# Head sums per token tile, squares of x from row-major x, and an early load of the second batch's rows

## The chip, the cores and the metric

One core of a Trainium2 chip runs the kernel; the other cores have nothing to do with it. The metric is the time of one execution on the device in microseconds (us), as the median of several. Lower is better. The engines are called PE (TensorE), DVE (VectorE), ACT (ScalarE), POOL (GpSimd) and SP (SyncE, which issues most of the DMAs).

## What is computed

Two cross-attention layers over 16 batches of 512 tokens with 256 features. The first layer is the one that the change touches:

```python
def _L0_xattn_ref(x_tokens, ctx, ctx_index_per_token, gamma_q, gamma_kv, Wq, Wk, Wv, Wo):
    # B=16, T=512, K=64, D=256, H=16 heads of hd=16
    q = split(rmsnorm(x_tokens, gamma_q) @ Wq.T)
    kn = rmsnorm(ctx, gamma_kv)
    k = split(kn @ Wk.T)
    v = split(kn @ Wv.T)
    ctx_pos = jnp.arange(K)[None, None, :]
    mask = (jnp.abs(ctx_pos - ctx_index_per_token[:, :, None]) <= 1)[:, None]
    scores = jnp.einsum('bhqd,bhkd->bhqk', q, k) / math.sqrt(hd)
    w = jnp.square(jax.nn.relu(scores))
    w = jnp.where(mask, w, 0.0)
    denom = jnp.maximum(w.sum(-1, keepdims=True), EPS_DEN)
    out = jnp.einsum('bhqk,bhkd->bhqd', w / denom, v)
    return x_tokens + out.reshape(B, T, D) @ Wo.T
```

The second layer takes that result as its queries: it projects, applies gelu, scores it against the 64 context rows of its batch, takes a softmax, adds the result to its input and applies a layer norm.

## The kernel before, in words

Because of the mask a token looks at three context rows only: that of its own index (CENTRE), the next (UP) and the one before (DOWN). The kernel picks these rows by matmuls with a one-hot matrix. The queries of layer 0 are not normalised: w stays unscaled, and the floor under the denominator is scaled instead, by the sum of squares of each token's x. So for each token and head three products are needed (query times picked key, summed over the 16 features of the head), and for each token the sum of x squared.

**Head sums.** The products lie in the tile `qk`, features over partitions (two groups g of 128) and 512 tokens along the free axis, one slice of 1024 elements per shift. `head_sums` (L571 to L579) sums over the features of a head with a selection matrix of 32 columns. The PE array is used in four groups of 32 columns: three of them take one shift each, the fourth takes the squares of x (`xsq`), and each streams 512 tokens. The result fills bank 0 of the PSUM: quarter s of the partitions holds shift s, the last quarter the floor. ACT moves it to `s_sb` with a Relu and adds a small bias in the floor's row (L1049), PE turns it by four transposes of 128x128 (L640) so that tokens lie on partitions, ACT squares the three shifts in place (L1061), and DVE sums them to `den`, takes the maximum with the floor in PSUM (`dcl`, L1327), the reciprocal (L1329) and the weights `wn` (L1331). `xsq` is made by ACT in `square_x` (L1004 to L1007): one Square over the whole 128x1024 slice of `x_ring`, where x lies features over partitions.

**The pipeline.** `steps` (L216) runs 16 steps. In a step five batches are under way: e is loaded, a gets its queries and picked keys, f its weights and picked values, b is projected to the second layer's queries and scored, n gets its softmax, layer norm and output. The order on each engine is written out by hand, in a function `step` per engine. What matters here is one round of PE and DVE. At the end of a PE step stand `head_sums(a)` and then, as the first thing of the next step, the eight transposes of the attended values (L635), which wait for DVE's sum of the three shifts (L1305, semaphore `sum_ready`). Behind them come the transposes of `s_sb` (L640), two transposes of the softmax (L648), half of the queries (L498 to L500), the output matmuls (L670), picked values UP (L549) and the projection of b (L498 to L500 on `o_hi`, `o_lo`). DVE waits for the projection in the second of its two residual additions (L1347, semaphore `xp_mm`). After that DVE makes `xp_lo` (L1350), the attended values (L1270, L1356), the products of the next batch (L1259), CENTRE values (L1270), the maxima of the scores (L1376) and again the sum L1305.

**The start.** PE computes keys and values for all 16 batches, two per tile t (0 to 7). ACT rounds them (L991, `round_keys_values`), DVE computes the remainder (L1221), and SP moves half of each tile across partitions (`cross`, L262 to L267, "the crossing"). ACT's list there is fixed: four sums of squares of the context rows (L963), `square_x(0)`, tiles 4 and 5, x of batch 1, tiles 6 and 7. After tile 7, DVE splits the weights of the second layer's values (`v_lo`, L1298), for which PE waits. SP issues the loads of x (`load`, L257 to L260), the crossings, and four shifted copies of the keys and values per batch (`shifted`, L269 to L279).

## Time and profile before

| | |
|---|---|
| median of 3 runs | 348.92 us (348.28 to 348.96) |
| the profiled execution, whole | 349.19 us |
| its span, first to last instruction | 347.4 us |
| PE busy in the span | 332.7 us, 96% |
| DVE busy | 307.8 us, 89% |
| ACT busy | 242.2 us, 70% |
| POOL busy | 169.7 us, 49% |
| mean granted clock of PE | 0.988 |
| DMA | 37.96 MB, mean 109 GB/s |

The span has three parts: the start to about 53 us, thirteen steps that repeat nearly alike, one every 18.2 us, and the end from about 307 us. Busy shares are averages over all three. A matmul's end is modelled in the profile, and matmuls overlap, so PE counts as busy up to the modelled end even where its next instruction waits. PEld is PE's loading of stationary operands, which can run ahead of the matmuls. Instructions that only wait or issue a DMA are not busy time. Times in the rows are microseconds from the start of the span.

### The profile page before, as it was taken

To read this page: it belongs to the slowest core of one execution; us is meant where nothing else is said; L and a number is where in the kernel's file an instruction comes from. 1 tells how busy PE (TensorE), PEld (TensorE's weight loads), DVE (VectorE), ACT (ScalarE), POOL (GpSimd) and SP (SyncE) were. 2 spreads that over 40 slices of the span, in tenths; PEclk is the share of its full clock that TensorE was granted. 3 is DMA by queue.
4 is the path that set the end of the run, shared out by engine and by line. 5 is a ranking of instruction groups with operands and counts; after the bars stand their busy time and mean duration, and the time that the engine had idled before them with its cause. 6 is when DMAs were issued, how large, how long until landed. Compare 5 with 4: busy or idle time off the path is not lost.

```text
span 347.4 us, 5599 instructions
## 1 busy us (share of the span) xinstructions
PE 332.7 (96%) x1930; PEld 240.7 (69%) x1930; DVE 307.8 (89%) x486; ACT 242.2 (70%) x486; POOL 169.7 (49%) x203
## 2 busy tenths in 40 slices
PE   7999999999999999999999999999999999999980
PEld 3575778868686767676868677776767686857750
DVE  1689598999999999999999989999999999999766
ACT  4599433486868695959595959596877868685752
POOL 4315020025656473839283747474747566444424
PEclk9899999999999999999999999999999999999997
DMA  7975615903232222323141414141414132010103
GB/s 238 315 219 149 199 57 131 248 17 129 83 117 94 102 98 79 109 66 126 63 149 60 152 61 151 62 150 62 150 63 144 67 133 80 2 60 2 60 0 122
DMA packets 21819, 37.96 MB, mean 109 GB/s; under 512 B 2144, under 2 KB 8288, under 8 KB 21792
## 3 DMA queue, kind: packets, MB, share of 16 engines
q1 hardware_dynamic: 18816, 29.48, 27.2%
q0 software_dynamic: 2016, 7.34, 6.1%
q10 hardware_dynamic: 960, 0.79, 0.7%
q8 instruction: 15, 0.25, 0.3%
q14 instruction: 12, 0.10, 0.1%
HBM read 16.77 MB, written 8.39 MB: 72 GB/s over the span
## 4 chain that ended last, share of the span: by engine, by line
PE 79%; DVE 13%; ACT 3%; DMA 2%; issue 1%; ACTq 0%; DVEq 0%
PE ps L498 12%; PE ps L499 12%; PE ps L500 12%; PE ps L577 7%; PE ps L549 7%; PE ps L543 6%; PE ps L635 4%; PE ps L670 4%; PE ps L752 4%; PE ps L743 4%; DMA vfd<-wv0T 2%; PE ps L530 2%; PE ps L640 2%; DVE qkp L1259 2%; DVE kv L1221 2%
## 5 line engine op out<-in xcount | busy, mean ns | idle before, releaser
L1259 DVE TENSOR_TENSOR qkp<-ps,bufs 128x1024 f32<-128x1024 f32 x48 | 55.7, 1215 | 0.9 <-PE ps L543 0.8
L377 POOL TENSOR_TENSOR x_lo<-x_ring,x_hi 128x1024 fp32r<-128x1024 f32 x16 | 38.0, 2373 | 37.7 <-ACT x_hi L998 37.7
L418 POOL TENSOR_TENSOR bufs<-bufs,lng_twice 128x1024 f32<-128x1024 f32 x14 | 33.8, 2411 | 28.3 <-ACT bufs L1038 26.2
L1076 ACT ACTIVATE xp_hi<-bufs 128x512 fp32r<-128x512 f32 x28 | 17.7, 632 | 41.1 <-DVE bufs L1347 41.1
L391 POOL TENSOR_TENSOR mean_gap<-stats 128x4 f32<-128x4 f32 x14 | 2.8, 198 | 72.0 <-DVE stats L1336 65.2
L1270 DVE TENSOR_TENSOR ps<-ps,wn 128x1024 f32<-128x1024 f32 x31 | 37.9, 1224 | 0.0
L420 POOL TENSOR_TENSOR bufs<-bufs,lnb_row 128x1024 f32<-128x1024 f32 x14 | 33.3, 2378 | 1.1
L577 PE MATMUL ps<-qkp,cst 128*32 128x512 f32 x192 | 30.7, 598 | 0.0
L577 PE MATMUL ps<-bufs,cst 128*32 128x512 f32 x64 | 30.5, 598 | 0.0
L1002 ACT ACTIVATE bufs<-ps 128x512 f32<-128x512 f32 x32 | 19.2, 603 | 16.1 <-PE ps L500 16.0
L498 PE MATMUL ps<-x_hi,wh_q 128*128 128x512 f32 x64 | 26.6, 415 | 0.0
L1038 ACT ACTIVATE bufs<-ps,nbias,half_rstd 128x256 f32<-128x256 f32 x52 | 25.0, 562 | 0.2
L499 PE MATMUL ps<-x_hi,wl_q 128*128 128x512 f32 x64 | 25.1, 392 | 0.0
L500 PE MATMUL ps<-x_lo,wh_q 128*128 128x512 f32 x64 | 25.1, 392 | 0.0
L498 PE MATMUL ps<-xp_hi,wh_q 128*128 128x512 f32 x60 | 23.8, 396 | 0.1
L498 PE MATMUL ps<-o_hi,wh_o 128*128 128x512 f32 x60 | 23.5, 392 | 0.0
L499 PE MATMUL ps<-xp_hi,wl_q 128*128 128x512 f32 x60 | 23.5, 391 | 0.0
L499 PE MATMUL ps<-o_hi,wl_o 128*128 128x512 f32 x60 | 23.5, 391 | 0.0
L500 PE MATMUL ps<-xp_lo,wh_q 128*128 128x512 f32 x60 | 23.5, 391 | 0.0
L500 PE MATMUL ps<-o_lo,wh_o 128*128 128x512 f32 x60 | 23.4, 389 | 0.0
L1347 DVE TENSOR_TENSOR bufs<-ps,x_ring 128x512 f32<-128x512 f32 x28 | 19.2, 686 | 3.9 <-PE ps L500 3.9
L1270 DVE TENSOR_TENSOR qkp<-ps,wn 128x1024 f32<-128x1024 f32 x16 | 19.4, 1210 | 3.4 <-PE ps L549 3.3
(257 smaller groups left out, 933.3 us busy)
## 6 DMA issues: line engine op xcount, KB each, us to landing
x_ring<-xT SPq DMA_DIRECT2D x16, 512.0 KB, 3.5
out<-bufs POOLq DMA_DIRECT2D x14, 512.0 KB, 3.4
idx_ring<-idx SPq DMA_DIRECT2D x16, 256.0 KB, 3.9
wkv_lo<-kv SPq DMA_DIRECT2D x32, 126.0 KB
kvs<-kv SPq DMA_DIRECT2D x30, 126.0 KB
vfd<-bufs SPq DMA_DIRECT2D x8, 256.0 KB, 4.5
qkp<-ctxT SPq DMA_DIRECT2D x2, 512.0 KB, 6.8
kv<-kv_cross SPq DMA_DIRECT2D x8, 128.0 KB, 4.1
```

Of the source, the lines that this page charges most:

```text
L377: G.tensor_tensor(x_lo[:, :, :], x_ring[:, e % RING, :, :], f32_view(x_hi[:, :, :]), ALU.subtract).then_inc(xl_ready, 2)
L418: G.tensor_tensor(zo, zn, lng_twice[:, :].unsqueeze(1).broadcast_to([P, TT, D]), ALU.mult).then_inc(zg_ready, 1)
L420: G.tensor_tensor(zo, zo, lnb_row[:, :].unsqueeze(1).broadcast_to([P, TT, D]), ALU.add).then_inc(zo_ready, 1)
L498: mm(o, hi, m_hi, start=start, stop=False)
L499: mm(o, lo, m_hi, start=False, stop=False)
L500: last = mm(o, hi, m_lo, start=False, stop=stop)
L543: i = mm(ps[:, bank0 + g, :], shift_rows(a, s, 0)[:, g * P:(g + 1) * P], onehot[:, a % 2, :], start=True, stop=True)
L549: i = mm(ps[:, bank0 + j // 2, (j % 2) * D:(j % 2 + 1) * D], onehot[:, f % 2, j * P:(j + 1) * P], shift_rows(f, s, 1), start=True, stop=True)
L577: i = mm(ps[32 * s:32 * s + 32, 0, :], sum_sel[:, g if s < SHIFTS else 2, :], qk[:, s, g, :] if s < SHIFTS else xsq[:, g, :], start=(g == ...
L1038: i = A(zn[:, j, :], out_rows(j), ACT.Identity, bias=nbias[:, j:j + 1], scale=half_rstd[:, j:j + 1])
L1259: V.tensor_tensor(qk[:, s, :, :], ps[:, bank0:bank0 + 2, :], q0, ALU.mult).then_inc(qk_ready, 1)
L1270: V.tensor_tensor(dst.rearrange("p a (h d) -> p (a h) d", d=HD), picked(bank0).rearrange("p a (h d) -> p (a h) d", d=HD), wn[:, s, :, :].r ...
```

## The change

`head_sums` is cut along the tokens instead of along the shifts: the four column groups take the four tiles of 128 tokens, and each matmul streams the three shifts of its tile, 3 x 128 = 384 columns. The squares of x are no longer an operand of PE. In their place x is loaded a second time, in rows (tokens over partitions, new tensor `x`, new tile `x_rows`, 512 KB for each batch), and ACT squares it in four instructions of 128x256 with an accumulator output into `floor`. DVE then adds the small constant to `floor` and takes the maximum with `den` in one instruction. The Relu moves 384 columns instead of 512 and has no bias, there are three transposes instead of four (one per shift), and the weights lie in another order in PSUM.

`load_rows(i)` on SP waits until the squares of the batch before are done. `load_rows(0)` stands behind the context rows in the start, `load_rows(1)` between the third and the fourth crossing, and the others at the end of SP's step, behind the shifted copies. `square_x` waits for the rows and no longer for the head sums of the batch before.

```diff
-C_ID, C_SEL, C_POS, C_EPS, C_END = 0, 128, 224, 225, 226
+FLOOR_SCALE = (16.0 * EPS_DEN / D) ** 0.5
+C_ID, C_SEL, C_POS, C_END = 0, 128, 192, 193
...
-        xsq, q0, xpT, q1T = (bufs[:, n, :].rearrange("p (c t) -> p c t", c=DC) for n in (0, 3, 4, 5))
+        q0, xpT, q1T = (bufs[:, n, :].rearrange("p (c t) -> p c t", c=DC) for n in (3, 4, 5))
+        x_rows = bufs[:, 0, :].rearrange("p (j d) -> p j d", j=TT)
+        floor = sb("floor", [P, 2, TT])
...
-        by_token = ps[:, 0, :].rearrange("p (j r) -> p j r", j=TT)
-        w = by_token[:, :, 0:32 * SHIFTS].rearrange("p j (s h) -> p s j h", h=32)[:, :, :, 0:H]
-        den_floor = by_token[:, :, 96:97]
+        by_shift = ps[:, 0, 0:SHIFTS * P]
+        w = by_shift.rearrange("p (s j h) -> p s j h", s=SHIFTS, h=32)[:, :, :, 0:H]
...
+            def load_rows(i):
+                if i > 0:
+                    sp.wait_ge(floor_ready, TT * i)
+                sp.dma_start(x_rows, x[i].rearrange("(j p) d -> p j d", p=P)).then_inc(rows_in, 16)
...
             context_rows()
+            load_rows(0)
             weight(raw["v1"], wv1, wv1_in)
...
             cross(3)
+            load_rows(1)
             cross(4)
...
                     shifted(e)
+                if e is not None and e >= 2:
+                    load_rows(e)
...
             def head_sums(a):
                 pe.wait_ge(qk_ready, 3 * a + 3)
-                pe.wait_ge(xsq_ready, a + 1)
                 for g in range(DC):
-                    for s in range(SHIFTS + 1):
-                        i = mm(ps[32 * s:32 * s + 32, 0, :], sum_sel[:, g if s < SHIFTS else 2, :],
-                               qk[:, s, g, :] if s < SHIFTS else xsq[:, g, :], start=(g == 0), stop=(g == DC - 1))
+                    for j in range(TT):
+                        i = mm(ps[32 * j:32 * j + 32, 0, 0:SHIFTS * P].rearrange("p (s t) -> p s t", s=SHIFTS), sum_sel[:, g, :],
+                               qk[:, :, g, j * P:(j + 1) * P], start=(g == 0), stop=(g == DC - 1))
                 i.then_inc(s_mm, 1)
...
-                    for j in range(TT):
-                        i = nc.tensor.transpose(ps[:, 0, j * P:(j + 1) * P], s_sb[:, j * P:(j + 1) * P], ident)
+                    for s in range(SHIFTS):
+                        i = nc.tensor.transpose(ps[:, 0, s * P:(s + 1) * P], s_sb[:, s * P:(s + 1) * P], ident)
...
             def square_x(a):
-                if a > 0:
-                    act.wait_ge(s_mm, a)
-                A(xsq, x_ring[:, a % RING, :, :], ACT.Square).then_inc(xsq_ready, 1)
+                act.wait_ge(rows_in, 16 * a + 16)
+                if a > 1:
+                    act.wait_ge(dcl_ready, a - 1)
+                for j in range(TT):
+                    A(x_rows[:, j, :], x_rows[:, j, :], ACT.Square, scale=FLOOR_SCALE,
+                      accum_out=floor[:, a % 2, j:j + 1]).then_inc(floor_ready, 1)
...
-                    A(s_sb[:, :], ps[:, 0, :], ACT.Relu, bias=den_eps).then_inc(s_cp, 1)
+                    A(s_sb[:, 0:SHIFTS * P], by_shift, ACT.Relu).then_inc(s_cp, 1)
...
-                    V.tensor_tensor(dcl[:, :, :], den[:, :, :], den_floor.broadcast_to([P, TT, H]), ALU.max).then_inc(dcl_ready, 1)
+                    dve.wait_ge(floor_ready, TT * f + TT)
+                    V.scalar_tensor_tensor(dcl[:, :, :], floor[:, f % 2, :].unsqueeze(2).broadcast_to([P, TT, H]), 16.0 * EPS_DEN * EPS_RMS,
+                                           den[:, :, :], ALU.add, ALU.max).then_inc(dcl_ready, 1)
```

The same edits are made in the code for the last batch. How the instructions stand now is shown at three places. The first is PE at the end of a step: the last rows of the scores, the head sums (`32x512` is 32 output rows, 512 columns) and the first transposes of the next step. Before:

```order
L756 MATMUL ps<-cst,scT 128x128 [waits scT_cp]
L756 MATMUL ps<-cst,scT 128x128
L577 MATMUL ps<-qkp,cst 32x512 [waits xsq_ready,qk_ready]
L577 MATMUL ps<-qkp,cst 32x512 x2
L577 MATMUL ps<-bufs,cst 32x512
L577 MATMUL ps<-qkp,cst 32x512 x3
L577 MATMUL ps<-bufs,cst 32x512
L635 MATMUL ps<-cst,qkp 128x128 [waits sum_ready]
L635 MATMUL ps<-cst,qkp 128x128 x7
L640 MATMUL ps<-cst,s_sb 128x128 [waits s_cp]
```

The same place now, with the line numbers of the changed kernel:

```order
L766 MATMUL ps<-cst,scT 128x128 [waits scT_cp]
L766 MATMUL ps<-cst,scT 128x128
L587 MATMUL ps<-qkp,cst 32x384 [waits qk_ready]
L587 MATMUL ps<-qkp,cst 32x384 x7
L645 MATMUL ps<-cst,qkp 128x128 [waits sum_ready]
L645 MATMUL ps<-cst,qkp 128x128 x7
L650 MATMUL ps<-cst,s_sb 128x128 [waits s_cp]
L650 MATMUL ps<-cst,s_sb 128x128 x2
```

Still eight matmuls in four column groups, each of 384 columns now, and three transposes of `s_sb` in place of four; the wait of the turn for `sum_ready` stays where it was.

The second place is ACT in the start: the sums of squares of the context rows, the squares of x of batch 0, and the rounding of tile 4. Before:

```order
L963 ACTIVATE scT,cms<-bufs 128x256 [waits ctx_in]
L963 ACTIVATE scT,cms<-bufs 128x256 [waits cms_done] x3
L1007 ACTIVATE bufs<-x_ring 128x1024
L991 ACTIVATE kv<-ps,crs 64x512 [waits crs_done,kv_mm]
L991 ACTIVATE wh_q<-ps,crs 64x512
```

Now:

```order
L973 ACTIVATE scT,cms<-bufs 128x256 [waits ctx_in]
L973 ACTIVATE scT,cms<-bufs 128x256 [waits cms_done] x3
L1019 ACTIVATE bufs,floor<-bufs 128x256 [waits rows_in]
L1019 ACTIVATE bufs,floor<-bufs 128x256 x3
L1001 ACTIVATE kv<-ps,crs 64x512 [waits crs_done,kv_mm]
L1001 ACTIVATE wh_q<-ps,crs 64x512
```

One Square has become four with a wait for the loaded rows, ahead of the same rounding.

The third place is SP in a middle step, now: the load of x and of the indices, the four shifted copies, the rows.

```order
L261 DMA x_ring<-xT 128x2x512 [waits x_in,idx_in,onehot_ready,xp_ready]
L262 DMA idx_ring<-idx 128x512
L285 DMA wkv_lo<-kv 63x512 [waits kvs_in_1,vg_mm,kv_in_2,kvs_zero_1]
L286 DMA wkv_lo<-kv 63x512
L285 DMA wkv_lo<-kv 63x512
L286 DMA wkv_lo<-kv 63x512
L267 DMA bufs<-x 128x4x256 [waits floor_ready]
```

The last row is new; the six before it stand as they did.

## Rows read from the trace of the kernel before

**Rows 1.** The profile's page: the chain that ended last, by engine.
```profile
PE 79%; DVE 13%; ACT 3%; DMA 2%; issue 1%; ACTq 0%; DVEq 0%
```

**Rows 2.** One step by engine: stretch, length, busy time of each engine, clock, DMA.
```profile
core 0: us, PE busy (x) PEld busy (x) DVE busy (x) ACT busy (x) POOL busy (x), PEclk, DMA share, GB/s
...
144.04:162.27 18.23, 18.23 (x115) 13.27 (x118) 17.22 (x27) 13.84 (x29) 10.79 (x14) 1.00 0.31 101
```

**Rows 3.** Waits: engine, line, releaser: us in total, times, longest us.
```profile
PEld ps L635 <- DVE qkp L1305: 11.6, 13, 0.9
```

**Rows 4.** Timeline, DVE, one step: start, duration, line, operation, count, idle before.
```profile
144.63 1.21 DVE L1305 TENSOR_TENSOR qkp<-ps,qkp 128x1024 f32<-128x1024 f32 x1
...
148.81 0.22 DVE L1327 TENSOR_TENSOR dcl<-den,ps 128x64 f32<-128x64 f32 x1
...
153.56 0.69 DVE L1347 TENSOR_TENSOR bufs<-ps,x_ring 128x512 f32<-128x512 f32 x1 [0.26 <-PE ps L500]
154.16 1.48 DVE L1350 TENSOR_TENSOR xp_lo<-bufs,xp_hi 128x512 fp32r<-128x512 f32 x2
...
162.81 1.21 DVE L1305 TENSOR_TENSOR qkp<-ps,qkp 128x1024 f32<-128x1024 f32 x1
```

**Rows 5.** Timeline, PE, the same step.
```profile
144.85 0.60 PE L577 MATMUL ps<-qkp,cst 128*32 128x512 f32 x3
...
145.28 0.61 PE L577 MATMUL ps<-qkp,cst 128*32 128x512 f32 x3
...
145.90 1.09 PE L635 MATMUL ps<-cst,qkp 128*128 128x128 f32 x8
146.83 0.60 PE L640 MATMUL ps<-cst,s_sb 128*128 128x128 f32 x4
147.26 0.38 PE L648 MATMUL ps<-cst,enf 128*128 128x128 f32 x2
...
153.13 0.39 PE L500 MATMUL ps<-o_lo,wh_o 128*128 128x512 f32 x1
```

**Rows 6.** Timeline, PE, the step before the repeating ones: last head sums.
```profile
52.45 0.60 PE L577 MATMUL ps<-qkp,cst 128*32 128x512 f32 x3
```

**Rows 7.** Timeline, PEld, the same place: what is loaded behind the head sums.
```profile
52.99 1.59 PEld L530 LDWEIGHTS ps<-wf_raw,bufs 128*128 128x128 f32 x8 [0.84 <-issue]
```

**Rows 8.** Timeline, ACT, in the middle step.
```profile
149.56 1.05 ACT L1007 ACTIVATE bufs<-x_ring 128x1024 f32<-128x1024 f32 x1
153.33 0.63 ACT L1076 ACTIVATE xp_hi<-bufs 128x512 fp32r<-128x512 f32 x1 [2.72 <-DVE bufs L1347]
```

**Rows 9.** Timeline, ACT, in the start.
```profile
23.35 0.42 ACT L963 ACTIVATE scT<-bufs 128x256 f32<-128x256 f32 x1
...
23.89 0.42 ACT L963 ACTIVATE scT<-bufs 128x256 f32<-128x256 f32 x1
...
24.31 1.04 ACT L1007 ACTIVATE bufs<-x_ring 128x1024 f32<-128x1024 f32 x1
25.87 0.69 ACT L991 ACTIVATE kv<-ps,crs 64x512 fp32r<-64x512 f32 x1 [0.52 <-POOL crs L373]
```

**Rows 10.** The chain that ended last, in order of time, in the start.
```profile
35.34 0.70 DVE v_lo L1298
...
36.08 0.50 PE ps L498
```

**Rows 11.** DMA in the start, stretches as in rows 2.
```profile
14.00:16.00 2.00, 2.00 (x6) 1.04 (x5) 1.85 (x3) 0.92 (x3) 0.97 (x1) 0.83 1.08 342
16.00:18.00 2.00, 2.00 (x11) 1.62 (x10) 1.97 (x6) 1.95 (x3) 0.00 (x0) 1.00 0.41 106
```

**Rows 12.** Timeline, POOL, around the same middle step.
```profile
135.97 0.20 POOL L407 TENSOR_TENSOR nbias<-nmean,half_rstd 128x4 f32<-128x4 f32 x1
...
143.46 2.38 POOL L377 TENSOR_TENSOR x_lo<-x_ring,x_hi 128x1024 fp32r<-128x1024 f32 x1
...
154.16 0.74 POOL L407 TENSOR_TENSOR nbias<-nmean,half_rstd 128x4 f32<-128x4 f32 x1
```

More of the change, by code:

```diff
@@ L43, in xattn_pair @@
         ident = cst[:, C_ID:C_ID + P]
-        sum_sel = cst[:, C_SEL:C_SEL + 96].rearrange("p (g c) -> p g c", g=3)
+        sum_sel = cst[:, C_SEL:C_SEL + 64].rearrange("p (g c) -> p g c", g=DC)
         pos = cst[:, C_POS:C_POS + 1]
-        den_eps = cst[:, C_EPS:C_EPS + 1]
         vec = sb("vec", [P, 5, DC])
@@ L134, in xattn_pair @@
             "vec_in", "cst_in", "wk1_in", "wkv_in", "wq0_in", "wv1_in", "wf1_in", "w1_in", "ln_in", "x_in", "idx_in"))
+        rows_in = sem("rows_in")
         ctxT_in = [sem("ctxT_in0"), sem("ctxT_in1")]
@@ L145, in xattn_pair @@
         kv_first = sem("kv_first")
-        onehot_ready, xsq_ready, xh_ready, xl_ready = map(sem, ("onehot_ready", "xsq_ready", "xh_ready", "xl_ready"))
+        onehot_ready, floor_ready, xh_ready, xl_ready = map(sem, ("onehot_ready", "floor_ready", "xh_ready", "xl_ready"))
         q0_mm, q0_cp, kg_mm, qk_ready, s_mm, s_cp, sT_mm, w_ready = map(sem, (
@@ L773, in last_weights @@
                 pe.wait_ge(s_cp, LAST + 1)
-                for j in range(TT):
-                    i = nc.tensor.transpose(ps[:, 0, j * P:(j + 1) * P], s_sb[:, j * P:(j + 1) * P], ident)
+                for s in range(SHIFTS):
+                    i = nc.tensor.transpose(ps[:, 0, s * P:(s + 1) * P], s_sb[:, s * P:(s + 1) * P], ident)
                 i.then_inc(sT_mm, 1)
@@ L1059, in step @@
                     act.wait_ge(sT_mm, f + 1)
-                    by_row = w.rearrange("p s j h -> p j s h")
+                    by_row = w.rearrange("p s j h -> p (s j) h")
                     A(by_row, by_row, ACT.Square).then_inc(w_ready, 1)
@@ L1113, in last_sums @@
                 act.wait_ge(s_mm, LAST + 1)
-                A(s_sb[:, :], ps[:, 0, :], ACT.Relu, bias=den_eps).then_inc(s_cp, 1)
+                A(s_sb[:, 0:SHIFTS * P], by_shift, ACT.Relu).then_inc(s_cp, 1)
             def last_squares():
                 act.wait_ge(sT_mm, LAST + 1)
-                by_row = w.rearrange("p s j h -> p j s h")
+                by_row = w.rearrange("p s j h -> p (s j) h")
                 A(by_row, by_row, ACT.Square).then_inc(w_ready, 1)
@@ L1399, in last_weights @@
                 dve.wait_ge(den_ready, LAST + 1)
-                V.tensor_tensor(dcl[:, :, :], den[:, :, :], den_floor.broadcast_to([P, TT, H]), ALU.max).then_inc(dcl_ready, 1)
+                dve.wait_ge(floor_ready, TT * LAST + TT)
+                V.scalar_tensor_tensor(dcl[:, :, :], floor[:, LAST % 2, :].unsqueeze(2).broadcast_to([P, TT, H]), 16.0 * EPS_DEN * EPS_RMS,
+                                       den[:, :, :], ALU.add, ALU.max).then_inc(dcl_ready, 1)
                 dve.wait_ge(dcl_ready, LAST + 1)
@@ L1601 @@
     arrays = {
-        "xT": a["x"].transpose(0, 2, 1), "ctx": ctx, "ctxT": ctx.T, "idx": a["itok_BxS_0_255"],
+        "xT": a["x"].transpose(0, 2, 1), "x": a["x"], "ctx": ctx, "ctxT": ctx.T, "idx": a["itok_BxS_0_255"],
         "vectors": np.stack([a[n].reshape(DC, P).T for n in ("L0_xattn_gamma_q", "L0_xattn_gamma_kv", "L1_xattn_bq",
```

4 lines of the change are left out of this document (1 added, 3 removed).

## The prediction

> **What bounds the kernel now.** I read four views, from coarse to fine: the page, the waits, the stretches, and the timelines of one step. The page's chain gives PE 79% of the span [rows 1], and in a middle step PE counts as busy for all 18.23 us of its stretch, against 17.22 us of DVE [rows 2]. Read alone, this says that every microsecond taken from PE is a microsecond won. The waits say otherwise at one place: in 13 of the steps the loading of weights for the turn of the attended values (L635), right behind the head sums, ends a wait for DVE's sum L1305 [rows 3]. The timelines show how tight this is. The sum runs from 144.63 for 1.21 us, so it ends at 145.84, and L635 starts at 145.90, 0.06 us later [rows 4, 5].
>
> Was PE ready then anyway? The last group of four head sums starts at 145.28 [rows 5]. One step earlier in the program the same head sums are followed by work that waits for nobody: there the last group starts at 52.45 and the next weights are loaded at 52.99, 0.54 us later [rows 6, 7]. So PE was ready for L635 at 145.28 + 0.54 = 145.82, and DVE let it go at 145.90. The two engines meet here almost to the instant, and DVE is the later one.
>
> From there I follow the loop that sets the period. PE works from L635 (145.90) to the end of the projection's last matmul, 153.13 + 0.39 = 153.52: 7.62 us. DVE, which had stood idle for 0.26 us, starts its second residual addition at 153.56 [rows 4, 5]. From there to the end of the next sum (162.81 + 1.21 = 164.02) DVE needs 10.46 us. With the two hand-overs of 0.04 and 0.06 us the round is 7.62 + 0.04 + 10.46 + 0.06 = 18.18 us, which is the distance of the sums, 162.81 - 144.63 [rows 4]. **The head sums are not in this loop.** They run while DVE does its 10.46 us. PE's other loop, in which they are, is as long only by coincidence.
>
> **The change part by part.**
>
> Head sums: the four column groups start together, and such groups of four follow each other at 145.28 - 144.85 = 0.43 us [rows 5]. With 384 columns for 512 I take three quarters, 0.32 us. Four groups per batch save 0.43 us. Bounds: 0 if a group's time does not follow the columns (its moving operand now is three runs of 128), 0.43 if it does; I take 0.43 since the columns are what it streams. In the 13 steps that wait at L635, PE now arrives 0.43 us earlier and waits that much longer: nothing won. In the step before them it counts, because no one waits for DVE there [rows 6, 7]: PE is on the path from 36.08 [rows 10] until the first of the residual additions that wait for it. So 0.43 us, once.
>
> Transposes of `s_sb`: four take 147.26 - 146.83 = 0.43 us [rows 5], one of them 0.11. They lie behind the wait, inside PE's 7.62 us, so the one that goes shortens the loop: 13 steps and the one before, 14 x 0.11 = 1.54 us. What would be late next there is DVE: it had 0.26 us idle before the second addition [rows 4], so it is ready when PE comes 0.11 earlier, even if nothing else moves. Two more of these transposes go off the path for nothing: batch 0's before 36.08, where PE waits for `v_lo` [rows 10], and the last batch's, where the chain has left PE for DVE and ACT.
>
> Relu over 384 columns, no bias: its result is wanted by the transposes L640 only, behind eight others. Shorter, never later: 0.
>
> `square_x`, middle steps: one Square of 1.05 us becomes four of 128x256 with an accumulator. Such instructions follow each other at 23.89 - 23.35 = 0.54 us where they wait for one another, and the last is followed by the next instruction after 24.31 - 23.89 = 0.42 us [rows 9]. So four take 1.7 to 2.2 us, 0.6 to 1.1 more. Behind them on ACT stands the rounding of the second layer's queries, `xp_hi`, before which ACT idles 2.72 us, waiting for DVE [rows 8]. That covers it. Were this cover gone, `xp_hi` would be late by the excess and `xp_lo` on DVE with it, inside the loop. 0.
>
> `square_x(0)`, start: the same 0.64 to 1.12 us stand ahead of the rounding of tile 4, and there ACT idled only 0.52 us, waiting for POOL [rows 9]. The rounding comes 0.12 to 0.60 us later, and DVE's remainders and `v_lo`, for which PE waits at 36.08 [rows 10], can be late by all of it or by nothing, as DVE still has the products of batch 0 to do. Bounds 0 and +0.60; I take +0.10, near the low end, since these four do not wait for one another and so go at 0.42.
>
> DMAs: `load_rows(0)` puts 512 KB into SP's queue ahead of four weights. The queue's engines are full until 16 us (342 GB/s in 14 to 16) and idle by more than half after that (106 GB/s in 16 to 18) [rows 11]; 512 KB at 342 GB/s are 1.5 us. The weights behind it land that much later; the first of them is wanted by the split that ends in `v_lo` at 35.34 [rows 10]. The first copies of keys and values are issued at that time too, and PE wants the shifted ones some microseconds later. Bounds 0 and +1.5; I take 0, since the queue drains before these copies are all issued. `load_rows(1)` waits for ACT's squares between two crossings, where SP waits for later tiles anyway; nothing is queued behind it that could have gone. In the middle steps the rows are the last DMA of SP's step, and ACT wants them a whole step later. 0.
>
> DVE: `dcl` (0.22 us at 148.81 [rows 4]) becomes one instruction with two operations and reads the floor from SBUF. Its wait is for squares a step old. Between it and the loop's hand-over lies the 0.26 us of idle time, so up to that it costs nothing in the steps, and once, at the end, whatever it is longer. The sums over shifts now stride 128 words in place of 32. Bounds 0 and +0.3 in all; I take 0.
>
> One rule speaks against this edit. At 154.16 DVE runs `xp_lo`, with both inputs in SBUF, and POOL's small L407, issued at the same moment, takes 0.74 us, where it took 0.20 a step before [rows 4, 12]: POOL was held. If this works both ways, `dcl`, which had one input in PSUM and now has both in SBUF, can be held by POOL's instructions of 2.38 us [rows 12]. The Trainium skill ("SBUF — State Buffer", section "SBUF: two separate sides") states the rule that a DVE instruction with two SBUF inputs and a GpSimd instruction that reads SBUF share a port pair as an exclusive lock, so that the loser is blocked for the whole instruction. By that rule, the trace agrees for POOL's side; DVE's side no row here shows. I take 0 for it, because POOL's last long one ends at 143.46 + 2.38 = 145.84 and `dcl` starts at 148.81 [rows 4, 12].
>
> Sum: -0.43 - 1.54 + 0.10 = **-1.87 us**. The profiled execution took 349.19 us, 0.27 over the median, so I take the difference to the median: 348.92 - 1.87 = 347.05, rounded 347.0. Its own bounds: -1.97 without the cost of the start; with the start at +0.60, `dcl` and the sums longer by 0.3 and no gain in the columns, -1.54 + 0.90 = -0.64.
>
> **The rivals.** (A) *PE is the bound, as page and chain say.* Then each of 14 steps gives 0.43 + 0.11 = 0.54 us: -7.6, or 341.4 us. For it: PE busy without a gap [rows 2], PE 79% of the chain [rows 1]. Against: L635 starts 0.06 us after DVE's sum [rows 4, 5], and PE's arrival does not make that sum earlier. Chance 0.05.
>
> (B) *The gain is lost elsewhere.* The transpose is worth 0.11 us a step only while DVE has its 0.26 us idle [rows 4]. If the strided sums and the new `dcl` together take over 0.26 us more, DVE sets the pace before the residual addition too, and the result lies between -0.7 and +0.7 us: 348.9. Against: same elements, same engine. Chance 0.15.
>
> (C) *Slower, by the lock.* If POOL's long instructions come to lie over `dcl`, each step waits up to 2.38 us, less the 0.26 of idle time: 2.1 us in 14 steps, up to +30 us, 378. The point from which it decides: POOL would have to end its x_lo 148.81 - 145.84 = 3.0 us later in the step than now, and up to 0.26 us of overlap costs nothing. Half a microsecond of overlap gives 0.24 x 14 = 3.4 us, and 348.92 - 1.87 + 3.4 = 350.4. Chance 0.05; I add 0.03 for the start with every upper bound at once, -0.64 + 1.5 = +0.9, 349.8.
>
> (D) *The change does nothing,* head sums as long as before and the transpose hidden: 348.9, counted in B.
>
> **How the numbers follow.** The forecast has 0.72, A 0.05, B with D 0.15, C 0.08. A measurement of this kernel can tell about 0.2%, 0.7 us, from no change. Of the forecast's 0.72 nearly all lies below 348.2; I leave 0.02 to no change. Faster 0.75, same 0.16, slower 0.09. The forecast with its bounds is 346.9 to 348.3. The range may leave out 0.2, which are A, C and the upper half of B; so it reaches into B, to 348.8, and on the fast side I give it 1.1 us, for idle times inside the loop that shrink with PE's new slack: 345.8 to 348.8.
>
> **What would show each step right or wrong.** Groups of four head sums at 0.32 us. The wait of L635's weights for DVE's sum longer by about 0.4 us in each middle step, PE busy for some 17.6 us of a round of 18.07 us. First `xp_hi` still after an idle stretch of 1.6 us or more. PE's start behind `v_lo` at 36.1 to 36.7. `dcl` at 0.2 to 0.3 us. I am wrong if the round is 17.7 us or less (A), if it stays at 18.18 (B), if `dcl` takes microseconds (C), or if the start moves by more than 0.6 us.

## The result, and the profile after

| | before | after |
|---|---|---|
| median | 348.60 us (4 runs, 348.01 to 348.96) | 345.12 us (4 runs, 344.85 to 345.12) |
| profiled execution, its span | 349.19 us, 347.4 us | 344.85 us, 343.1 us |
| one round of the repeating steps | 18.17 us | 18.04 us |

The changed kernel is faster by 3.5 us, ratio 0.990 (95% interval 0.9883 to 0.9917). Beside the experiments below the kernel before was timed 77 times more, with a median of 348.05 us; against that the change is worth 2.9 us. The 0.6 to 0.9 us between the baselines are taken up below, under the half clock. A round is the distance from the first to the last sum of the repeating steps, divided by 13: before 71.93 and 308.14, after 69.45 and 304.02.

The middle of the kernel went as forecast. The same stretch by engine, PE, PEld, DVE, ACT and POOL with their busy time, clock and DMA share; here the last round, beside [rows 2]:

```profile
286.16:304.20 18.04, 17.64 (x117) 13.13 (x109) 17.17 (x27) 13.37 (x35) 10.52 (x14) 1.00 0.08 31
```

The waits (in all, times, longest), beside [rows 3]:

```profile
PEld ps L645 <- DVE qkp L1318: 14.3, 13, 1.1
...
PE ps L645 <- DVE qkp L1318: 5.3, 13, 0.4
```

The page's chain, beside [rows 1]:

```profile
PE 42%; DVE 39%; issue 9%; ACT 6%; DMA 2%; ACTq 0%; DVEq 0%
```

PE is no longer busy without a gap (17.64 us of 18.04), and the matmuls of the turn now wait 0.4 us in each of 13 steps for DVE's sum. The chain, which before gave PE 79%, now goes to PE for one half of the round and to DVE for the other: the loop of the two half rounds, which the page had hidden behind a PE that came 0.08 us early, has become visible. (The turn is the eight transposes of the attended values, now L645.) The timeline of PE at that place (start, duration, line, count, idle before), beside [rows 5]:

```profile
285.72 1.13 PE L587 MATMUL ps<-qkp,cst 128*32 128x384 f32 x9
287.25 1.09 PE L645 MATMUL ps<-cst,qkp 128*128 128x128 f32 x8 [0.40 <-DVE qkp L1318]
288.18 0.49 PE L650 MATMUL ps<-cst,s_sb 128*128 128x128 f32 x3
288.51 0.38 PE L658 MATMUL ps<-cst,enf 128*128 128x128 f32 x2
```

And of DVE in that round, beside [rows 4]; the last row is of ACT, beside [rows 8]:

```profile
285.98 1.22 DVE L1318 TENSOR_TENSOR qkp<-ps,qkp 128x1024 f32<-128x1024 f32 x1
...
290.17 0.23 DVE L1341 SCALAR_TENSOR_TENSOR dcl<-floor,den 128x64 f32<-128x64 f32 x1
...
294.77 0.69 DVE L1362 TENSOR_TENSOR bufs<-ps,x_ring 128x512 f32<-128x512 f32 x1 [0.24 <-PE ps L511]
...
304.02 1.22 DVE L1398 TENSOR_TENSOR qkp<-ps,qkp 128x1024 f32<-128x1024 f32 x1
```

```profile
294.56 0.63 ACT L1089 ACTIVATE xp_hi<-bufs 128x512 fp32r<-128x512 f32 x1 [2.07 <-DVE bufs L1362]
```

The three transposes take 288.51 - 288.18 = 0.33 us for the 0.43 of four. `dcl` takes 0.23 us, DVE's idle time before the second addition is still 0.24 us, and ACT still idles 2.07 us before the first `xp_hi`, where it had 2.72.

What is not explained by this is the start. At the matmul for which PE waited on `v_lo` [rows 10], PE is at 34.15 us now, where it was at 36.08: 1.93 us earlier, where the prediction had 0.1 us later. The experiments are about this, and about whether the reasons given for the rest hold.

### The profile page after: what moved, and what is told of

It is laid out like the page before. It is cut to its first block, busy times and chain, and to the rows that moved or that the text cites. A ratio compares the mean times of both kernels' runs of the same rounds, so it can differ in the third digit from the quotient of the medians.

```text
span 343.1 us, 5709 instructions
## 1 busy us (share of the span) xinstructions
PE 323.1 (94%) x1914; PEld 237.6 (69%) x1914; DVE 307.0 (90%) x486; ACT 250.0 (73%) x598; POOL 171.5 (50%) x203
## 4 chain that ended last, share of the span: by engine, by line
PE 42%; DVE 39%; issue 9%; ACT 6%; DMA 2%; ACTq 0%; DVEq 0%
DVE qkp L1272 14%; DVE ps L1283 9%; PE ps L509 7%; PE ps L511 7%; PE ps L510 7%; PE ps L645 4%; DVE qkp L1318 4%; PE ps L680 4%; PE ps L560 3%; DVE bufs L1362 3%; ACT xp_hi L1089 3%; PE ps L541 2%; DMA vfd<-wv0T 2%; DVE nmax L1391 2%; PE ps L494 2%
## 5 line engine op out<-in xcount | busy, mean ns | idle before, releaser
L1019 ACT ACTIVATE bufs<-bufs 128x256 f32<-128x256 f32 x64 | 25.6, 405 | 0.0
L587 PE MATMUL ps<-qkp,cst 128*32 128x384 f32 x256 | 24.0, 492 | 0.0
```

The source lines that it names most:

```text
L1019: A(x_rows[:, j, :], x_rows[:, j, :], ACT.Square, scale=FLOOR_SCALE, accum_out=floor[:, a % 2, j:j + 1]).then_inc(floor_ready, 1)
```

## The experiments

Sixteen kernels ran. All but five are the changed kernel with one edit; e6, e8, e10, e12 and e13 start from the kernel before. The kernel before was timed beside each group on the same chip: 348.02, 348.04, 348.14 and 348.04 us in the medians. The changed kernel was not timed beside them and is taken at the 345.12 us of its own measurement; e7 and e16, which turned out to change nothing, came at 344.98 and 344.93, so differences to it are good to some 0.2 us.

### The loop: e1, e2, e3

The fourth transpose back, on columns that nobody reads:

```diff
-                    for s in range(SHIFTS):
+                    for s in range(SHIFTS + 1):
                         i = nc.tensor.transpose(ps[:, 0, s * P:(s + 1) * P], s_sb[:, s * P:(s + 1) * P], ident)
```

> The changed kernel with a fourth transpose of s_sb in each step (128 unused columns, its result is read by nobody). Loop theory (the round is PE from the turn to the projection plus DVE from the residual to the sum): each round 0.11 us longer again, 18.04 to 18.15 us, time 345.1 + 14 x 0.11 = 346.6 us. Rival 'the gain per round is something else (shorter Relu, DVE's sums, the squares on ACT)': less than +0.5 us. Rival 'PE is the bound': +1.5 us too, so this run does not tell PE-bound from the loop; the next two do.

Measured: 346.56 us, +1.4; the round is (305.74 - 69.70) / 13 = 18.16 us, 0.11 more. The transpose is worth what the prediction gave it, and it is nearly all of what a round gained (0.13 to 0.14 us).

Longer head sums, by four matmuls ahead of them that are overwritten (C = 64 in e2, 128 in e3):

```diff
+                for j in range(TT):
+                    mm(ps[32 * j:32 * j + 32, 0, 0:SHIFTS * C].rearrange("p (s t) -> p s t", s=SHIFTS), sum_sel[:, 0, :],
+                       qk[:, :, 0, j * P:j * P + C], start=True, stop=True)
                 for g in range(DC):
```

> The changed kernel with head sums lengthened by four matmuls of 3 x 64 columns, about 0.36 us of PE for each batch, overwritten at once. Loop theory: PE arrives at the turn 0.36 us later and waits 0.36 us less for DVE (0.40 to 0.04 us); the round stays at 18.04 us; only the steps without a wait pay, once or twice 0.36: 345.5 to 345.9 us. PE-bound rival: 15 x 0.36 = +5.4 us, 350.5 us.

Measured: 345.73 us, +0.6, round 18.06 us. PE's extra third of a microsecond disappears in the wait; the rival by which PE is the bound, +5.4 us, is gone.

> The changed kernel with head sums lengthened by four matmuls of 3 x 128 columns, about 0.72 us of PE for each batch. Loop theory: the wait of 0.40 us is used up, and the remaining 0.72 - 0.40 to 0.47 = 0.25 to 0.32 us go into each of 13 rounds (18.3 us), and 0.72 once or twice: 345.1 + 3.3 to 4.2 + 0.7 to 1.4 = 349.1 to 350.7 us. PE-bound rival: 15 x 0.72 = +10.8 us, 356 us. If the wait for DVE grows with it, neither: +1 us or less.

Measured: 348.77 us, +3.65, round 18.24 us. Twice the length costs six times as much: the wait is used up and the rest enters each round. The round grew by 0.19 us, less than the 0.25 to 0.32 expected, because the four matmuls took 0.64 us and not 0.72 (in e5, below, PE's next work starts 2.07 us after the head sums' start, for 1.43 after the change). So the threshold lies at 0.64 - 0.19 = 0.45 us: the 0.40 of the wait and a little more. In the last round of e3 DVE's sum ends at 290.75 and the turn starts at 290.98, 0.23 us later, where the hand-over after the change is 0.05. This is the clearest evidence for the loop: the same edit in two sizes, on both sides of the point from which it decides.

### The start: e5, e14, e6, and a better row of before

The same four matmuls with C = 128, in the head sums of batch 0 alone (e5) and, with a == 1, of batch 1 alone (e14):

```diff
+                for j in range(TT if a == 0 else 0):
```

> The changed kernel with the head sums of batch 0 alone, in the start, lengthened by four matmuls of 3 x 128 columns (0.72 us of PE, once). New theory for what the forecast missed in the start: there PE, not DVE's v_lo, is the late one or level with it, so the head sums of batch 0 are on the path: +0.7 us, 345.8 us. The prediction's account (PE waits there for v_lo, what it saves ahead of it is free): +0.0 to +0.1 us, 345.1 to 345.2 us. In between, if v_lo takes over as the later one: not possible for a lengthening.

Measured: 345.43 us, +0.3 to +0.45. Two profiles whose starts are level (the one-hot matrix of batch 0 at 14.49 in e5 and in e15, whose edit acts in the repeating steps only) give it closer: DVE's sum before the first turn stands at 50.92 and 50.44, 0.48 us apart. The head sums of batch 0 are on the path, for three quarters of the 0.64 us. The prediction had them at nothing.

> The changed kernel with the head sums of batch 1 alone lengthened by 0.72 us, in the step before the repeating ones. The prediction's account and the loop theory agree: nothing waits there for DVE, so it costs its full length once: +0.6 to +0.7 us, 345.7 to 345.8 us. If it is hidden: 345.1 us.

Measured: 345.69 us, +0.6; the first turn starts at 53.17, against 52.53 in e15. Those of batch 1 count in full, as forecast.

From the profile of before to that of after DVE's rounding of `v` had shrunk from 1.31 to 0.52 us, and in both POOL's clearing of the shifted copies was near it. e6 takes it away from there, in the kernel before:

```diff
             pool.wait_ge(kv_mm, CT)
+            pool.wait_ge(v1_ready, 1)
             clear_shifted(1)
```

> The kernel before with one wait more: POOL clears the second buffer of shifted copies (2.78 us, SBUF to SBUF) only when DVE's rounding v_hi and its remainder v_lo are done. In the profile of before the rounding took 1.31 us under that clearing, after the change 0.52 us beside its last 0.23 us. Theory 'the gain in the start is the freed rounding': the rounding takes 0.42 to 0.5 us, v_lo ends 0.8 us earlier, and the time falls by 0.3 us (as PE waited only 0.3 us there) up to 0.8 us: 347.2 to 347.7 against 348.0. Rival 'PE's own work and the stretch at half clock made the difference': the rounding is short, and the time stays at 348.0 within 0.15 us.

Measured: 348.01 us beside 348.04: nothing. The theory of the freed rounding falls. Why, another kernel shows, e10 (below): its instructions are those of the kernel before up to 74 us. PE and DVE in its start:

```profile
33.10 0.60 PE L646 MATMUL ps<-cst,s_sb 128*128 128x128 f32 x4
...
33.15 0.51 DVE L1302 CAST v_hi<-vfd 128x512 fp32r<-128x512 f32 x1
33.70 0.69 DVE L1304 TENSOR_TENSOR v_lo<-vfd,v_hi 128x512 fp32r<-128x512 f32 x1
...
34.93 0.40 PE L504 MATMUL ps<-o_hi,v_hi 128*128 128x512 f32 x1
```

The rounding takes 0.51 us without any edit there, `v_lo` ends at 34.39, and PE comes to use it at 34.93, without an idle stretch. In this execution DVE is half a microsecond early and PE is the late one, so the head sums of batch 0 are on the path. After the change the two are level again:

```profile
33.41 0.69 DVE L1311 TENSOR_TENSOR v_lo<-vfd,v_hi 128x512 fp32r<-128x512 f32 x1
...
34.15 0.50 PE L509 MATMUL ps<-o_hi,v_hi 128*128 128x512 f32 x1
```

`v_lo` ends at 34.10 and PE uses it 0.05 us later, so this is as far as PE's gain goes. The fourth transpose of batch 0 is worth nothing measurable there: between the profiles of after and e1 the one-hot matrix of batch 0 moves from 14.44 to 14.55 and DVE's sum before the first turn from 50.38 to 50.51, which leaves 0.02 us for it.

The wait of PE at 36.08 [rows 10], from which the prediction concluded that PE is early there, is in none of the profiles of e6, e8, e10, e12 and e13, all made from the kernel before: in these PE comes 0.46 to 0.63 us behind `v_lo`.

### The half clock: e12, e13

The two executions differ in PE's clock between 11 and 15 us. Windows of both, with PE's clock in the column behind POOL; the kernel before as profiled:

```profile
10.00:12.00 2.00, 1.62 (x3) 0.82 (x4) 1.37 (x5) 1.64 (x3) 1.05 (x1) 0.81 1.07 376
12.00:14.00 2.00, 2.00 (x4) 0.70 (x3) 0.32 (x1) 1.09 (x2) 1.38 (x1) 0.50 1.10 346
```

and e10:

```profile
10.00:12.00 2.00, 1.86 (x7) 1.05 (x7) 1.42 (x5) 1.59 (x3) 1.05 (x1) 1.00 1.07 375
12.00:14.00 2.00, 2.00 (x6) 0.80 (x6) 1.16 (x3) 1.82 (x3) 1.32 (x1) 1.00 1.10 348
```

In the profile of before, PE ran at the lower of its two levels, 1.2 GHz, from 11.3 to 14.7 us, after it had idled for 0.67 us ahead of 10.38; in e10 it idled for 0.15 us at that place. Eight matmuls took 5.40 us there, and 3.70 in e10 and after the change. What the 1.7 us do further on can be followed in the two profiles. ACT's rounding of tile 4 starts at 25.87 for 24.23 in e10, and POOL's clearing, which comes right behind POOL's `x_lo` and so waits for ACT's `x_hi`, at 32.24 for 30.61. PE makes up half of it and has its transposes of `s_sb` at 33.93 for 33.10. So the clearing, which in e10 ends at 33.38, 0.23 us after the rounding has begun, lies over the rounding until 35.02, the rounding takes 1.31 us, and `v_lo` is late by 1.64 us where PE is late by 0.8.

Of the 77 executions of the kernel before beside the experiments, 21 took over 348.4 us, up to 349.8, while most lie at 348.0; the profiled one took 349.19. They fall into two sorts: eight at 349.3 to 349.8 us with a mean granted clock of 0.987 to 0.988, like the profiled one (0.988), and thirteen at 348.5 to 348.8, eleven of them with 0.984 to 0.985, of which no profile was taken. Kernels made from the changed one have such executions too (e1: seven at 346.4 to 346.7 us, two at 347.4). So about 1 us of the difference between the two profiles is not the change, and a baseline of three runs, two of them at 348.9, stands 0.9 us above the usual execution.

Does the lower clock come from the wait? Both runs fill it with matmuls of zeros, in the kernel before:

```diff
             context_sums()
+            for _ in range(2):
+                mm(ps[:, 1, :], s_sb[:, 0:P], s_sb[:, :], start=True, stop=True)
```

> The kernel before with two more matmuls on PE (zeros, unused result, 0.9 us) where it waits 0.67 us for the folded weights at 9.7 us. The profile of before shows PE at half clock (1.2 GHz) from 11.3 to 14.7 us, after that wait; runs of 348.0 us do not, runs of 348.6 to 349.4 us may. Theory 'the half clock follows from the wait': no execution above 348.4 us, median 348.0 to 348.3. If the half clock comes whatever PE does there: the same mixture as the kernel before, a fifth of the executions above 348.4 us.

Measured: 348.89 us, the 12 executions between 348.77 and 349.41. The filling took 1.8 us until the next matmul, not 0.9, since one such matmul of 512 columns takes 0.9 us; it delayed what follows by more than a microsecond (14.94 for 13.57 in e10), at a clock of 1.00 throughout, and the run settles nothing. With one matmul of 256 columns, which took 0.68 us:

```diff
             context_sums()
+            mm(ps[:, 1, 0:256], s_sb[:, 0:P], s_sb[:, 0:256], start=True, stop=True)
```

> The kernel before with one matmul of 256 columns of zeros (0.46 us) on PE in its wait of 0.4 to 0.67 us at 9.7 us. If the half clock behind that wait follows from the wait: the executions fall together, none above 348.4 us, median 347.9 to 348.2. If not: about a fourth of the executions at 348.6 to 349.4 us, as in the 62 executions of the kernel before so far.

Measured: 348.09 us, and all 11 executions between 347.98 and 348.33. If 21 in 77 lie above 348.4 us by chance whatever PE does, eleven without one have a chance of 3%; by the rate of the kernel before beside this run, 3 in 15, it is 9%, and for the eight like the profiled one it is 30%. And e6 and e10, which start as the kernel before does and fill nothing, have two such executions in 22. A wait is not enough either: in e4 PE idled for 0.57 us at the same place, and its clock stayed at 1.00. So the wait is a possible cause of the half clock, and no run here shows it. The median stays, so for the usual execution the filling is worth nothing.

### The lock: e7, e9, e10, e15, e16

e7 lays the clearing over DVE's rounding in the changed kernel:

```diff
             pool.wait_ge(kv_mm, CT)
+            pool.wait_ge(kv_lo_done, 2 * CT - 1)
             clear_shifted(1)
```

> The changed kernel with POOL's clearing held back until DVE is at the last remainder, so that it lies over the rounding v_hi, which reads and writes SBUF. Lock theory: the rounding cannot go before POOL ends, it takes 2.2 to 2.5 us in place of 0.52, v_lo ends 1.8 us later and PE waits for it: +1.5 to +1.9 us, 346.6 to 347.0 us. No lock (both run side by side): +0 to +0.2 us. If DVE holds the port instead, POOL's clearing takes longer and the shifted copies are late: under +0.5 us.

Measured: 344.98 us, nothing. The timeline of e7, POOL and DVE:

```profile
32.32 2.78 POOL L366 TENSOR_SCALAR wkv_lo<-minus_half 128x1024 fp32r<-128x1024 f32 x1 [1.73 <-DVE kv_cross L1235]
...
32.98 0.66 DVE L1310 CAST v_hi<-vfd 128x512 fp32r<-128x512 f32 x1
...
33.67 0.69 DVE L1312 TENSOR_TENSOR v_lo<-vfd,v_hi 128x512 fp32r<-128x512 f32 x1
...
34.28 1.10 DVE L1264 TENSOR_SCALAR onehot<-idx_ring,cst 128x512 fp32r<-128x512 int32 x1
```

The rounding is 0.23 us longer than in e6 (0.43 us), `v_lo` is as long as ever, and only the one-hot matrix is held, 1.10 for 0.48 us, to 0.28 us after POOL's end. In the profile of before the rounding also ended 0.28 us after POOL (33.99 + 1.31 against 32.24 + 2.78), and so it did in e10 (33.66 against 33.38), in e12 (35.02 against 34.74) and, at 0.29, after the change (33.37 against 33.08). Only in e7, where the clearing had another 2.1 us to go as the rounding began, was it not held.

So `v_lo`, with two SBUF inputs, was not held. Is then rival C of the prediction idle? e9 puts a POOL instruction over `dcl`; e10 is the same edit in the kernel before, where `dcl` reads the floor from PSUM:

```diff
                 if n is not None:
+                    if f is not None:
+                        pool.wait_ge(ln_in, 16 * 2)
+                        pool.wait_ge(w_ready, f + 1)
+                        G.tensor_tensor(bufs[:, 2, :].rearrange("p (j d) -> p j d", j=TT),
+                                        lng_row[:, :].unsqueeze(1).broadcast_to([P, TT, D]),
+                                        lnb_row[:, :].unsqueeze(1).broadcast_to([P, TT, D]), ALU.add)
                     norm_factors(n)
```

> The changed kernel with one more POOL instruction in each of 13 steps: a sum of two SBUF rows, 128x1024, into unused SBUF, started when ACT's squares are done, that is 0.4 us before dcl, and 2 to 2.5 us long. It is rival C of the prediction put on purpose. Exclusive lock (an instruction of DVE with two SBUF inputs, as dcl now is, cannot start before POOL ends): dcl takes 0.22 plus some 2 us, less the 0.24 us of idle time: 13 x 1.8 = +23 us, about 368 us. What the rounding under the clearing showed (v_lo with two SBUF inputs ran 0.69 us under POOL's clearing as it does alone; only the two copies with one input were lengthened): dcl 0.2 to 0.3 us, and 345.1 to 346 us.

> The same POOL instruction in the kernel before, where dcl has one input in PSUM. Exclusive lock by two SBUF inputs: dcl stays at 0.22 us here, time at 348.0 to 348.5 us; the difference to the run on the changed kernel is what the move of the floor to SBUF can cost. If any DVE instruction on SBUF is held (the reciprocal too): both kernels lose alike. No lock: 348.0 us, and both runs alike in their difference to their kernels, 0 to 0.5 us.

Measured: e9 358.68 us in the median of three executions, +13.6 (a fourth took 1800 us, which I can't explain), e10 348.05 us, nothing. The two instructions in e9:

```profile
283.10 2.37 POOL L443 TENSOR_TENSOR bufs<-lng_row,lnb_row 128x1024 f32<-128x1024 f32 x1 [1.15 <-ACT ps L1080]
...
283.85 1.70 DVE L1347 SCALAR_TENSOR_TENSOR dcl<-floor,den 128x64 f32<-128x64 f32 x1
```

and in e10:

```profile
292.26 2.37 POOL L432 TENSOR_TENSOR bufs<-lng_row,lnb_row 128x1024 f32<-128x1024 f32 x1 [1.47 <-ACT ps L1067]
...
293.01 0.22 DVE L1333 TENSOR_TENSOR dcl<-den,ps 128x64 f32<-128x64 f32 x1
```

The new `dcl` ends 0.08 us after POOL; the old one does not notice it. The change did buy this risk. Each round is longer by 1.04 us: 1.47 us of `dcl`, less DVE's idle 0.24, less 0.18 by which the two `xp_lo` come closer together (1.29 us for 1.47). The +23 us expected was too high because POOL had already run for 0.75 us when `dcl` came.

e15 and e16 ask which POOL instruction holds DVE. They are e9 with another instruction at its place; in e15 (`...` stands for its arguments, shown above):

```diff
-                        G.tensor_tensor(...)
+                        G.tensor_scalar(bufs[:, 2, :], minus_half[:, 0:1].broadcast_to([P, 4 * D]), 0.5, None, ALU.add)
```

In e16 the input is `lng_row`, repeated as in e9.

> As the run with POOL's sum over dcl, but POOL does a clearing (one column of SBUF, repeated, plus a constant; about 2.8 us) instead of a sum of two rows. If only a POOL instruction with two SBUF inputs holds DVE: dcl 0.22 us, 345.1 us. If every POOL instruction on SBUF holds a DVE instruction with two SBUF inputs: dcl 2.0 us, 362 us.

> The same with one real input row of 256 elements (repeated four times, plus a constant). Two-inputs rule: dcl 0.22 us, 345.1 us. Every-instruction rule: dcl 1.7 to 2.0 us, 358 to 362 us.

Measured: 345.49 us (two executions, 344.94 and 346.04, the second at a mean granted clock of 0.987 for 0.991) and 344.93 us (two). The rows of e16, where POOL reads one whole row of 256 elements:

```profile
289.66 2.80 POOL L443 TENSOR_SCALAR bufs<-lng_row 128x1024 f32<-128x1024 f32 x1 [1.32 <-ACT ps L1080]
...
290.40 0.38 DVE L1347 SCALAR_TENSOR_TENSOR dcl<-floor,den 128x64 f32<-128x64 f32 x1
```

`dcl` takes 0.38 us in both, 0.15 more than alone, and is not held. The POOL instruction that holds it has two SBUF inputs; under the two that have one, DVE is hardly slowed. The instruction of e9 is also of another kind (TENSOR_TENSOR, not TENSOR_SCALAR), and no run separates the kind from the number of inputs. The Trainium skill ("SBUF — State Buffer", section "Who interferes with whom") says that a DVE instruction with two SBUF inputs contends with a GpSimd instruction that reads SBUF. The rows of e9 agree. In e16 POOL reads SBUF too, and all that shows are 0.15 us under an instruction of 2.80; the measurement decides, for the instructions tried here.

### Using the freed time: e4, e8, e11

The wait of 0.40 us can be filled. In e4 the first two matmuls of the queries, which need only `x_hi`, come ahead of the turn; in e11 only the first does (early = 1):

```diff
+                early = 2 if a is not None and b is not None else 0
+                if early:
+                    pe.wait_ge(xh_ready, 2 * a + 2)
+                    for k, part in enumerate(list(weight("q0", 0, 0))[0:early]):
+                        mm(ps[:, Q0_BANKS[0], :], part, x_hi[:, 0, :], start=(k == 0), stop=False)
                 if b is not None:
...
-                    queries0(a, 0)
+                    queries0(a, 0, early)
```

`queries0` leaves out the first `early` matmuls in its turn; that part of the edit is not shown.

> The changed kernel with two of the six matmuls of the first half of the queries (those that need only x_hi, 2 x 0.23 us) issued ahead of the turn instead of behind it, so that they fill PE's wait of 0.40 us. Loop theory: 0.46 us leave the loop, 0.06 are lost ahead of it, but DVE idles only 0.24 us before the residual addition, so 0.24 to 0.40 us a round are won: 13 x 0.24 to 0.40 = -3.1 to -5.2 us, 340 to 342 us, and what DVE waits for afterwards is the new bound. PE-bound rival: PE has the same work, 345.1 us. If DVE's other idle places only grow: 344 to 345 us.

Measured: 342.24 us, -2.9; round 17.82 us, 0.23 less. That is all of DVE's idle time before the addition, as the lower bound said. The new bound is DVE:

```profile
286.45 1.29 DVE L1340 TENSOR_TENSOR o_lo<-ps,o_hi 128x512 fp32r<-128x512 f32 x2 [0.30 <-ACT o_hi L1078]
...
291.62 1.30 DVE L1370 TENSOR_TENSOR bufs<-ps,x_ring 128x512 f32<-128x512 f32 x2
```

The additions follow each other without a gap, and a wait of 0.30 us for `o_hi` has come up, since PE now reaches the turn 0.31 us after the sum's end.

> The kernel before with the same two matmuls of the queries moved ahead of the turn as in the run on the changed kernel. There PE's wait is 0.08 us, not 0.40: PE comes to the turn 0.38 us late, and gains 0.46 us behind it. Loop theory: the round falls by 0.08 us only, -1.0 us in 13 rounds, 347.0 us, against -2.9 us for the same edit on the changed kernel; that is, the time that the narrower head sums free is real but can be used only by work moved into it. If the edit is worth the same on both kernels (-2.9 us, 345.1), the head sums' length is irrelevant even so.

Measured: 349.62 us, **+1.6, slower**, round 18.26 us. The size is uncertain: five of the ten executions lie at 349.13 to 349.34 us with a mean granted clock of 0.990 to 0.992, 1.3 us above the usual 348.0, and five at 349.9 to 350.6 with 0.986 to 0.988. By either count I had the sign wrong. My count took the matmuls' place ahead of the turn off against their place behind it, and forgot who is waiting: DVE gets the delay of the turn and can use of the gain behind it only the time for which it idled. Its rows in e8:

```profile
293.06 1.29 DVE L1327 TENSOR_TENSOR o_lo<-ps,o_hi 128x512 fp32r<-128x512 f32 x2 [0.65 <-ACT o_hi L1065]
...
298.22 1.42 DVE L1355 TENSOR_TENSOR bufs<-ps,x_ring 128x512 f32<-128x512 f32 x2
```

`o_lo` starts 3.13 us after the sum's start, for 2.60 in e10: 0.53 us lost to the new wait. Won back are 0.44 us: 0.17 from the first addition to `xp_lo` (1.38 for 1.55, the idle time between the additions is gone), 0.22 from `o_lo` to the statistics (2.70 for 2.92), and 0.05 at the two `xp_lo` (1.43 for 1.48). What is left are the 0.08 us of each round, 1.0 us in 13; the rest of the 1.3 comes before them (the first of the 13 sums stands at 70.87, for 70.66 in e10). The same edit is worth -2.9 us with the narrow head sums and +1.3 us with the wide ones, execution against like execution. So the head sums' 0.43 us per batch, worth nothing in the repeating steps by itself, is what makes this edit pay.

> The changed kernel with only one matmul of the queries ahead of the turn, in place of two. With two, PE came to the turn 0.3 us after DVE's sum, DVE waited 0.30 us for o_hi, and its idle time before the residual addition was gone: the round of 17.82 us was DVE's own. On the kernel before that turned into a loss. Theory: with one (0.23 us of the 0.40 us wait) the turn is late by under 0.1 us, DVE's wait for o_hi is under 0.1 us, a small idle time before the residual is back, and PE's 7.5 - 0.23 us set the round: 17.8 us, 342.0 to 342.3 us, level with two. If DVE's round was limited by the late turn alone and not by PE, it falls by up to 0.2 us more: 339.5 us.

Measured: 342.19 us, level with e4, round 17.83 us. One matmul less takes DVE's wait for `o_hi` away and gives 0.17 us of idle time before the addition back: PE sets the round again, and to go lower both halves would have to shrink. e4 and e11 beat both kernels, by 5.8 and 5.9 us against before (ratios 0.9834, interval 0.9811 to 0.9857, and 0.9826, interval 0.9807 to 0.9846).

## Why the prediction was right or wrong

The difference, taken between two executions at full clock: e10 up to its repeating steps is the kernel before, and its POOL instruction changes no time. Positions in us:

| | before (e10) | after | difference | step |
|---|---|---|---|---|
| one-hot matrix of batch 0, DVE | 14.74 | 14.44 | -0.30 | -0.30 |
| transposes of `s_sb`, batch 0 | 33.10 | 32.37 | -0.73 | -0.43 |
| DVE's sum before the first turn | 51.04 | 50.38 | -0.66 | +0.07 |
| first turn, the step before the 13 | 53.56 | 52.46 | -1.10 | -0.44 |
| DVE's sum, first of the 13 | 70.66 | 69.45 | -1.21 | -0.11 |
| DVE's sum, last | 307.01 | 304.02 | -2.99 | -1.78 |
| end of the span | 346.2 | 343.1 | -3.1 | -0.1 |

- **What bounds the kernel: right.** The loop of PE and DVE, with the head sums outside it, was read from a distance of 0.08 us between two rows, against a page that gave PE 79%. e2 and e3 show it on both sides of its threshold, and the wait after the change shows it directly.
- **The transpose, 0.11 us in each round: right**, by e1. The round gained 0.14 us here; the remaining 0.03 lies in PE's half and I don't assign it. 13 rounds gave 1.78 us for the 1.43 of this term.
- **Head sums once, in the step before: right**, 0.44 us for 0.43; e14 confirms that they count there.
- **The start: wrong, and the step that failed** is that PE waits for DVE's `v_lo` at 36.08, so that what PE saves ahead of it is worth nothing: "PE is on the path from 36.08", "batch 0's before 36.08, where PE waits for `v_lo`". On this ground the head sums of batch 0 got no term at all. They gave 0.43 us up to the transposes of `s_sb` (table), of which 0.36 arrive, and lengthening them costs (e5). In e10 `v_lo` ends 0.54 us before PE comes for it; after the change it lets PE go 0.05 us after its end, and PE's first matmul after such a stop is followed by the next after 0.34 us, where in e10 it is 0.23. That is how 0.07 us are lost again, and with them the fourth transpose of batch 0: for it alone "for nothing" came out right, but not for the reason given. The row was read rightly, but the wait of 0.15 us for PE stood on DVE's rounding, which in that execution was 0.8 us longer than in e10. A position on the path was settled by 0.15 us in a stretch where PE had shown half its clock 20 us earlier.
- **`square_x(0)`, +0.10: not visible.** The four squares took 1.6 us and ended as the scale of the next tiles came; ACT rounded tile 4 with no idle time left.
- **DMAs, 0: right** in so far as nothing on the path came late. The -0.30 us at the one-hot matrix is an earlier landing of a weight (`wv0T`): DVE's folding, which waits for it, starts at 8.94 for 9.23. The landing varies as much among the changed kernel and those made from it, 8.94 to 9.26 us; but nine of their twelve profiles have it by 9.05, and the six of the kernel before and those made from it not before 9.16. So a part may belong to the change. No run isolates it.
- **The size against the baseline.** -1.87 was set against 348.92. Between the two profiles at full clock the change is worth 3.1 us, 1.23 more than the forecast: 0.36 from batch 0's head sums, 0.35 from the rounds, 0.30 from the one-hot row, 0.11 at the end, 0.10 that did not come, 0.01 in the step before. In the medians it is worth 2.9 us against the usual 348.05. The other 0.87 us by which 345.12 lies under 347.05 are the baseline's, of which two in three executions were unusual ones: set against 348.05 the same sum and its range would have stood at 346.2, 344.9 to 347.9. That the measured time falls below the range is thus about half a matter of the change's size and half one of chance in the baseline.
- **Rivals.** A is refuted (e2). B did not come: idle time and `dcl` are as before. C has its mechanism shown (e9 against e10), with its condition: POOL's instructions with two SBUF inputs would have to come over `dcl`, and they end 3 us before.

## What to carry to other kernels

When the page calls an engine the bound, look for the place where it waits, however little, and sum the round through that wait: work outside the loop is free in both directions until the threshold, and an edit can be worth -2.9 or +1.3 us depending on which side of it the kernel stands. Time freed outside the loop is a reserve that pays only when work is moved into it. Where a position on the path hangs on 0.1 or 0.2 us in one profiled execution, look at the clock of the stretch and ask for a second execution before a term is set to nothing.

## What the runs showed of the hardware

- A DVE instruction of 0.23 us with both inputs in SBUF took 1.70 us under a POOL instruction with two SBUF inputs and ended 0.08 us after it; with one input in PSUM it took 0.22 us (e9, e10). Under POOL instructions (TENSOR_SCALAR) with one SBUF input it took 0.38 us (e15, e16).
- Under such a one-input POOL instruction of 2.8 us, DVE's rounding (SBUF to SBUF) took 1.31 us in the profile of before, up to 0.28 us after POOL's end, and 0.66 us in e7, for 0.43 us alone; the one-hot matrix took 1.10 for 0.48 us in e7, also to 0.28 us after the end. Why one is held to POOL's end and the other not stays open.
- Eight head-sum matmuls of 384 columns in four column groups take 1.43 us until the next work starts; 512 columns took 1.85 (30.39 - 28.54 in the start of before).
- PE's granted clock fell to the lower level from 11.3 to 14.7 us in the profile of before, after an idle time of 0.67 us, and eight matmuls took 5.40 us for 3.70; in e4 it stayed at the upper level after an idle time of 0.57 us at the same place.
